# Transposes of token rows and heads' outputs by VectorE and DRAM, and weighted values in adjoining PSUM banks

## The chip, the core and the metric

The kernel runs on one core of a Trainium2 chip. The metric is the device time of one execution in microseconds. Everything is computed in float32 except for the mask, which is bfloat16. PE is TensorE, DVE is VectorE, ACT is ScalarE, POOL is GpSimd and SP is SyncE, which here only issues DMAs.

## What is computed

The input is `x` of shape (8, 1024, 128). The program applies a block twice (`DEPTH = 2`), in this order of layers as the kernel counts them (L = 0 to 3): two local-attention layers (L = 0, 1), global attention, and two more local-attention layers (L = 2, 3). Cut to what matters, one local layer is:

```python
h = shift_token(x)                       # second half of the channels comes from the token before
q, k, v = split(h @ wqkv, 3)             # 8 heads of 64
q = l2norm(q) * qs; k = l2norm(k) * ksc
q, k = rotary_xpos(q, k)
sim = einsum('bhwid,bhwjd->bhwij', 8 * q, look_around(k))    # windows of 64, this one and the one before
o = softmax(where(mask, -max, sim)) @ look_around(v)
x = x + o @ wo
h = layernorm(shift_token(x)) * g + b    # then the MLP
a, g = split(h @ w1 + b1, 2)
x = x + (a * gelu(g)) @ w2 + b2
```

Before layers 0 and 2 an outer layer norm is applied to each token row; after layers 1 and 3 half of the result is added to the residual `X`.

## The kernel before

`X` and `Y` hold all tokens in SBUF, token on the partition, as 64 rows (`NT = 64`) of 128 tokens. A local-attention stage of a layer runs in slots: `local_slot(L, s)` exists once per engine, and in slot s the engine works on several tiles of 128 tokens at once. Tile s is at the softmax, tile s+2 at the transposes of its keys and queries, tile s+3 at the values, tile s+4 at the projection of queries and keys and at its rotary products, tile s-1 at the weighted values and tile s-2 at the output projection. Each engine runs its list in a fixed order, written out by hand; semaphores alone bind the engines together. The MLP follows in groups of 4 tiles (`mlp_slot`), and the last four groups also start the next layer.

PE's order in a slot is `scores(s)`, `weigh_values(s-1)`, `heads_transpose(s-2)` (L1174), `project_qk(s+4, 0)` (L1209), `project_v(s+3)` (L1226), `project_qk(s+4, 1)`, `project_out(s-2)` (L1237), `weights_transpose(s)` twice (L1257), `tokens_transpose(s+5)` (L1164), `keys_transpose(s+2)` (L1271) and `queries_transpose(s+2)` (L1284). Token rows are transposed by TensorE to a PSUM bank and copied to `hT` by ACT in two halves (`tokens`, L536 and L537; the second half is moved by one column, which is the token shift). The outputs of the heads, `o`, are transposed by TensorE to bank 5 and copied by ACT to `oT` (`outputs`, L543).

DVE's order is `maxima(s)` (two reductions, L747), `sums(s-1)` (two reciprocals, L755), `norms(s+2)` (L771), `shares(s-1)` (two products, L762), `queries(s+4)` (sine and cosine products, L733 and L738), `add_heads(s-2)` (L799), `keys(s+4)` (cosine, sum of squares L793, sine), and in layers 0 and 2 the statistics of one row of the outer norm (`moments`, L846, L850). POOL does `root(s+4)` (floor L444, power L447), `total(s+4)` (L452) and in layers 0 and 2, for as long as there are rows, `normalise` (L464, L468, L472) for one row. `root(t)` does not start its power before `norms(t-1)` is done, and `norms(t)` needs `root(t)` and `total(t)`.

SP issues two DMAs per slot, which lay out the values of the window before (`vprev`, L393 and L395), and in slots 48, 52 and 56 of a layer `load_tokens` (L374 to L376), which copies 8 rows of `Y` for the MLP, half of the channels moved by one partition.

The weighted values of a tile lie in PSUM banks 7 and 2.

## Time and profile before

| | us |
|---|---|
| median of 3 runs | 3096.68 |
| lowest, highest | 3094.66, 3098.7 |
| profiled execution | 3094.52 |
| its span, first to last instruction | 3092.7 |

Over the span PE is busy for 3015.1 us (97%), DVE 2570.3 (83%), ACT 2223.2 (72%) and POOL 1815.0 (59%). The clock granted to TensorE is 0.991 of full speed on average. Local attention of layers 0 to 3 fills roughly 50 to 550, 680 to 1220, 1750 to 2250 and 2400 to 2930 us, global attention 1330 to 1700. Engine busy shares are unions over time; a matmul's shown duration overlaps the next one's, so throughput is read from one start to the next.

### The profile page before, as it was taken

Reading aid. Unit: us, or ns where it says so; the run is one execution under the profiler, and the core shown is the slowest. Engines: PE = TensorE matmul, PEld = TensorE weight load, DVE = VectorE, ACT = ScalarE, POOL = GpSimd, SP = SyncE. Lnnn points to the kernel's source line nnn. Section 1 sums busy time; section 2 is a strip of 40 time slices with the busy share of each in tenths; the row PEclk is TensorE's granted clock in tenths of the full one; section 3 lists DMA queues with packets and bytes.
Section 4 is the critical chain, followed back from the end, with each engine's and each line's share of the span. In section 5 each row is a group of like instructions: output and inputs, shape, how many; then the busy total and the mean of one; then the engine's idle time right before and its main releaser. Section 6 shows DMA issues by size and latency. Waiting matters only on the chain.

```text
span 3092.7 us, 83968 instructions
## 1 busy us (share of the span) xinstructions
PE 3015.1 (97%) x31009; PEld 2183.9 (71%) x31009; DVE 2570.3 (83%) x5290; ACT 2223.2 (72%) x5488; POOL 1815.0 (59%) x1258
## 2 busy tenths in 40 slices
PE   7999999999999999989999699999999999999999
PEld 4777777667777777657777477777766677777766
DVE  7999888677888888869999599999866788888866
ACT  5888888437888888328889388888853688888832
POOL 8999997125666665540000599999721566666610
PEclk8999999999999999999999899999999999999999
DMA  5111112101111121200000011111221111111211
GB/s 122 33 35 35 33 36 54 43 19 35 33 35 35 33 44 43 50 4 1 1 1 1 18 35 37 34 33 37 48 49 21 32 33 37 33 33 44 47 39 51
DMA packets 140627, 107.20 MB, mean 35 GB/s; under 512 B 85225, under 2 KB 105666, under 8 KB 140226
## 3 DMA queue, kind: packets, MB, share of 16 engines
q1 hardware_dynamic: 140226, 101.83, 14.7%
q8 instruction: 255, 4.18, 0.6%
q14 instruction: 146, 1.20, 0.1%
HBM read 12.67 MB, written 4.19 MB: 5 GB/s over the span
## 4 chain that ended last, share of the span: by engine, by line
PE 91%; DVE 4%; issue 2%; ACT 1%; POOL 1%; SPq 0%; DMA 0%; DVEq 0%; ACTq 0%; POOLq 0%
PE psum L1209 14%; PE psum L1083 11%; PE psum L1186 8%; PE psum L1226 7%; PE psum L1237 7%; PE psum L1257 7%; PE psum L1140 6%; PE psum L1109 5%; PE psum L1174 5%; PE psum L1271 3%; PE psum L1284 3%; PE psum L1470 3%; PE psum L1446 3%; PE psum L1130 3%; PE psum L1456 2%
## 5 line engine op out<-in xcount | busy, mean ns | idle before, releaser
L447 POOL TENSOR_TENSOR rnorm<-ssq_floor,neg_half 128x16 f32<-128x16 f32 x256 | 750.4, 2931 | 438.9 <-DVE qkr L771 430.0
L522 ACT ACTIVATE shared<-psum,neg_max 128x128 f32<-128x128 f32 x2048 | 595.0, 396 | 38.1 <-DVE neg_max L747 38.1
L452 POOL TENSOR_TENSOR qk_cos<-qk_cos,qk_sin 128x1024 f32<-128x1024 f32 x256 | 607.0, 2371 | 0.0
L1209 PE MATMUL psum<-wqkv,hT 128*128 128x512 f32 x1024 | 534.5, 606 | 16.8 <-DVE qk_sin L733 10.1
L733 DVE TENSOR_TENSOR qk_sin<-psum,sin 128x512 f32<-128x512 f32 x512 | 350.9, 685 | 118.3 <-ACT sq L529 117.2
L738 DVE TENSOR_TENSOR qk_cos<-psum,cos 128x512 f32<-128x512 f32 x512 | 350.7, 685 | 78.7 <-ACT sq L529 78.5
L581 ACT ACTIVATE shared<-psum,b1g 128x512 f32<-128x512 f32 (+1 forms) x192 | 131.6, 686 | 353.8 <-PE psum L1083 349.6
L543 ACT COPY shared<-psum 128x512 f32<-128x512 f32 x256 | 150.1, 586 | 322.0 <-PE psum L1174 322.0
L747 DVE TENSOR_REDUCE neg_max<-psum 128x4 f32<-128x512 f32 x512 | 327.8, 682 | 36.6 <-PE psum L1142 24.4
L529 ACT ACTIVATE sq<-psum 128x512 f32<-128x512 f32 x512 | 334.1, 653 | 27.5 <-PE psum L1209 27.3
L1083 PE MATMUL psum<-shared,w1g 128*128 128x512 f32 (+1 forms) x768 | 345.6, 593 | 5.4 <-DVE shared L837 4.0
L1237 PEld LDWEIGHTS psum<-wo,shared 128*128 128x128 f32 x2048 | 267.4, 191 | 117.8 <-issue 117.1
L771 DVE TENSOR_TENSOR qkr<-qk_cos,rnorm 128x1024 f32<-128x1024 f32 x256 | 307.7, 1202 | 19.8 <-issue 19.1
L556 ACT COPY shared<-psum 128x512 f32<-128x512 f32 x512 | 306.2, 600 | 10.7 <-PE psum L1257 5.0
L793 DVE TENSOR_REDUCE ssq<-sq 128x16 f32<-128x1024 f32 x256 | 309.3, 1208 | 0.0
L1186 PE MATMUL psum<-v,shared 128*64 128x65 f32 x4096 | 293.6, 224 | 0.0
L1189 PE MATMUL psum<-vprev,shared 128*64 128x65 f32 x4096 | 293.4, 224 | 0.0
L1186 PEld LDWEIGHTS psum<-v,shared 128*64 128x64 f32 x4096 | 258.2, 137 | 46.4 <-issue 46.4
L1226 PE MATMUL psum<-wqkv,hT 128*128 128x512 f32 x512 | 282.8, 634 | 2.1 <-DVE qk_cos L738 2.1
L1209 PEld LDWEIGHTS psum<-wqkv,hT 128*128 128x128 f32 x1024 | 178.2, 194 | 150.7 <-issue 140.9
L1257 PE MATMUL psum<-ident,shared 128*128 128x128 f32 x2048 | 270.2, 273 | 7.3 <-ACT shared L522 3.9
L1237 PE MATMUL psum<-wo,shared 128*128 128x128 f32 x2048 | 271.1, 275 | 1.5 <-ACT shared L522 1.5
(131 smaller groups left out, 6585.9 us busy)
## 6 DMA issues: line engine op xcount, KB each, us to landing
vprev<-v SPq DMA_DIRECT2D x512, 130.0 KB, 2.3
shared<-Y SPq DMA_DIRECT2D x32, 256.0 KB
shared<-Y SPq DMA_DIRECT2D x32, 254.0 KB
out<-X SPq DMA_DIRECT2D x8, 512.0 KB, 3.7
X<-in_L_attn_x SPq DMA_DIRECT2D x7, 512.0 KB, 6.9
wqkv<-in_L_ffn_wqkv SPq DMA_DIRECT2D x4, 512.0 KB, 4.1
w<-in_L_ffn_w SPq DMA_DIRECT2D x4, 341.0 KB
wqkv<-in_L_ffn_wqkv SPq DMA_DIRECT2D x4, 256.0 KB, 4.2
```

Source lines behind the costliest of these rows:

```text
L447: nc.gpsimd.tensor_tensor(rnorm[:], ssq_floor[:], neg_half[:], ALU.pow).then_inc(rnorm_ready, 1)
L452: nc.gpsimd.tensor_tensor(both, both, qk_sin[:, t.m % 2, :], ALU.add).then_inc(sum_ready, 1)
L522: last = nc.scalar.activation(probs[:, c * P:(c + 1) * P], bank(3 + i, (c % 4) * P, (c % 4 + 1) * P), ACT.Exp, bias=neg_max[:, c:c + 1])
L529: nc.scalar.activation(sq[:, i * INNER:(i + 1) * INNER], bank(i), ACT.Square).then_inc(sq_ready, 1)
L733: nc.vector.tensor_tensor(y, x[:, :, ::-1, :], part.unsqueeze(1).to_broadcast([P, HEADS, 2, DH // 2]), ALU.mult).then_inc(rot_ready, 1)
L738: nc.vector.tensor_tensor(heads(qk_cos[:, t.m % 2, i * INNER:(i + 1) * INNER]), heads(bank(i)), cos[:, t.m, i:i + 1, :].to_broadcast([P, H ...
L1083: last = nc.tensor.matmul(bank(banks[half], rows=slice(0, size)), w1g[:, half * HID + lo:half * HID + lo + size], zT, start=True, stop=True)
L1186: nc.tensor.matmul(bank(bk, col, col + HD1, slice(WIN, P)), probsT[:, at_h + WIN:at_h + P], v[:, t.m % 4, h, :], start=True, stop=True)
L1209: nc.tensor.matmul(bank(i), hT[:, t.m * P:(t.m + 1) * P], wqkv[:, i * INNER:(i + 1) * INNER], start=True, stop=True).then_inc(qk_psum, 1)
L1226: nc.tensor.matmul(bank(v_bank(t)), hT[:, t.m * P:(t.m + 1) * P], wqkv[:, 2 * INNER:3 * INNER], start=True, stop=True).then_inc(v_psum, 1)
L1237: last = nc.tensor.matmul(bank(out_bank(t), 0, P), oT[:, c * P:(c + 1) * P], wo[:, c, :], start=(c == 0), stop=(c == INNER // P - 1))
L1257: last = nc.tensor.transpose(bank(6 + i, (c % 4) * P, (c % 4 + 1) * P), probs[:, c * P:(c + 1) * P], ident[:])
```

## The change

Token rows of tiles 5 to 63 of a layer are no longer transposed by TensorE. DVE transposes the 32x32 squares of a row of `Y` where they lie (`token_blocks`), SP stores the result in a DRAM scratch tensor and loads it back in four DMAs with the squares at their transposed places, straight into `hT`. The outputs of the heads go the same way for all but the last 6 tiles of a layer (`heads_blocks`, `store_heads`, `load_heads`); DVE writes its squares so that the four channel chunks lie interleaved, and `project_out` reads its stationary operand at every fourth element. ACT's copies for these tiles go. The weighted values lie in banks 6 and 7; maxima, reciprocals and shares of a tile become one instruction each. The statistics and normalisation of the outer norm handle two rows in every second slot. The shifted copy of `load_tokens` is split into 112 and 15 partitions. Some waits follow the new owners of the banks.

```diff
+SQUARE = 32
+EARLY = 5
+LAST = 6
+    blocks_out = nc.dram_tensor("token_blocks", [4, P, P], F32).ap()
+    heads_out = nc.dram_tensor("head_blocks", [2, P, INNER], F32).ap()
+        head_blocks = shared[:, 8 * N:9 * N].rearrange("p (q n) -> p q n", q=2)
+        o_T = shared[:, 9 * N:10 * N].rearrange("p (q n) -> p q n", q=2)
+        def by_dma(t):
+            return t.row < NT - LAST
         def out_bank(t):
-            return 5 if t.row >= NT - 6 else 3
+            return 3 if by_dma(t) else 5
@@ norm_units
-            return range(s + 14, s + 15) if 0 <= s and s + 14 < NT else None
+            return range(s + 14, s + 16) if s % 2 == 0 and s + 14 < NT else None
@@ SP
-                sp.dma_start(dst[1:P, :, HALF:P], src[0:P - 1, :, HALF:P]).then_inc(done, 16)
+                sp.dma_start(dst[1:113, :, HALF:P], src[0:112, :, HALF:P]).then_inc(done, 16)
+                sp.dma_start(dst[113:P, :, HALF:P], src[112:P - 1, :, HALF:P]).then_inc(done, 16)
+            def store_heads(t):
+                k = dma_count(t)
+                sp.wait_ge(head_blocks_ready, k + 1)
+                wait(sp, heads_in[k % 2], 64 * (k // 2))
+                sp.dma_start(heads_out[k % 2], head_blocks[:, k % 2, :]).then_inc(heads_stored[k % 2], 16)
+            def load_heads(t):
+                k = dma_count(t)
+                sp.wait_ge(heads_stored[k % 2], 16 * (k // 2 + 1))
+                wait(sp, attn_ready, before(t, 2))
+                squares = heads_out[k % 2].rearrange("(b i) (j x) -> i b j x", i=SQUARE, x=P)
+                for j in range(P // SQUARE):
+                    sp.dma_start(o_T[j * SQUARE:(j + 1) * SQUARE, k % 2, :].rearrange("i (b x) -> i b x", x=P),
+                                 squares[:, :, j, :]).then_inc(heads_in[k % 2], 16)
+            def store_blocks(t):
+                k = late_count(t)
+                sp.wait_ge(blocks_ready, k + 1)
+                wait(sp, blocks_in[k % 4], 64 * (k // 4))
+                sp.dma_start(blocks_out[k % 4], blocks[:, k % 2, :]).then_inc(blocks_stored[k % 4], 16)
+            def load_blocks(t):
...
+                for j in range(P // SQUARE):
+                    lo = t.m * P + (1 if j * SQUARE >= HALF else 0)
+                    sp.dma_start(hT[j * SQUARE:(j + 1) * SQUARE, lo:lo + P].rearrange("i (b c) -> i b c", c=SQUARE),
+                                 squares[:, :, j, :]).then_inc(blocks_in[k % 4], 16)
             def local_slot(L, s):
+                if t := late_tile(L, s + 6):
+                    store_blocks(t)
+                if t := late_tile(L, s + 5):
+                    load_blocks(t)
+                if (t := tile_at(L, s - 1)) and by_dma(t):
+                    store_heads(t)
                 ... the two copies to vprev ...
+                if (t := tile_at(L, s - 1)) and by_dma(t):
+                    load_heads(t)
@@ ACT local_slot
-                if not tail and (t := tile_at(L, s - 2)):
-                    outputs(t)
                 if t := tile_at(L, s):
                     exponents(t, 0)
-                if tail and (t := tile_at(L, s - 2)):
+                if (t := tile_at(L, s - 2)) and not by_dma(t):
                     outputs(t)
-                if s >= 0 and (t := tile_at(L, s + 5)):
-                    tokens(t)
@@ DVE
             def maxima(t):
-                for i in range(2):
-                    s = bank(3 + i).rearrange("p (h k) -> p h k", k=P)
-                    wait(dve, scores_ready, before(t, 0))
-                    wait(dve, probs_ready, before(t, 1, 2))
-                    nc.vector.tensor_reduce(neg_max[:, 4 * i:4 * i + 4], s, AX_X, ALU.max,
-                                            negate=True).then_inc(max_ready, 1)
+                scored = psum[:, 3 * BANK:5 * BANK].rearrange("p (h k) -> p h k", k=P)
+                wait(dve, scores_ready, before(t, 0))
+                wait(dve, probs_ready, before(t, 1, 2))
+                nc.vector.tensor_reduce(neg_max[:], scored, AX_X, ALU.max, negate=True).then_inc(max_ready, 1)
+            def heads_blocks(t):
+                k = dma_count(t)
+                dve.wait_ge(o_ready, t.n + 1)
+                wait(dve, heads_stored[k % 2], 16 * (k // 2))
...
+                nc.vector.transpose(head_blocks[:, k % 2, :].rearrange("p (j n c) -> p j c n", j=4, c=4),
+                                    o.rearrange("p (c j n) -> p j c n", c=4, j=4)).then_inc(head_blocks_ready, 1)
+            def token_blocks(t):
...
+                if k > 1:
+                    dve.wait_ge(blocks_stored[(k - 2) % 4], 16 * ((k - 2) // 4 + 1))
+                nc.vector.transpose(blocks[:, k % 2, :], Y[:, t.row, :]).then_inc(blocks_ready, 1)
@@ DVE local_slot
                 if t := tile_at(L, s - 1):
                     shares(t)
+                    if by_dma(t):
+                        heads_blocks(t)
...
+                if t := late_tile(L, s + 7):
+                    token_blocks(t)
@@ PE
             def weigh_values(t):
-                    bk = (7, 2)[h // 4]
+                    bk = 6 + h // 4
             def project_out(t):
-                wait(pe, oT_ready, before(t, 0))
+                if by_dma(t):
+                    k = dma_count(t)
+                    pe.wait_ge(heads_in[k % 2], 64 * (k // 2 + 1))
+                    squares = o_T[:, k % 2, :].rearrange("p (x c) -> p c x", c=INNER // P)
...
+                    heads_c = squares[:, c, :] if by_dma(t) else oT[:, c * P:(c + 1) * P]
             def weights_transpose(t, i):
-                elif i == 1:
-                    wait(pe, o_ready, before(t, 1, 2))
+                else:
+                    wait(pe, o_ready, before(t, 1))
@@ PE local_slot, slots 1 to 59
                     weigh_values(tile(-1))
-                    if t := tile(-2):
-                        heads_transpose(t)
...
-                    if t := tile(5):
-                        tokens_transpose(t)
```

## Rows read from the trace of the kernel before

**Rows 1.** Stages: us; busy PE, PEld, DVE, ACT, POOL; clock, DMA share, GB/s.
```profile
200.00:300.00 100.00, 100.00 (x1258) 75.05 (x1258) 90.81 (x183) 83.01 (x229) 94.73 (x73) 1.00 0.15 34
...
2500.00:2600.00 100.00, 100.00 (x1243) 75.06 (x1243) 87.18 (x157) 83.26 (x231) 66.40 (x37) 1.00 0.15 34
```

**Rows 2.** Timeline of PE (start us, us, instruction), layer 3, one slot.
```profile
2504.75 0.66 PE L1174 MATMUL psum<-ident,shared 128*128 128x128 f32 x4
2505.24 1.02 PE L1209 MATMUL psum<-wqkv,hT 128*128 128x512 f32 x2
...
2507.90 1.05 PE L1237 MATMUL psum<-wo,shared 128*128 128x128 f32 x8
2508.79 1.04 PE L1257 MATMUL psum<-ident,shared 128*128 128x128 f32 x8
2509.66 0.27 PE L1164 MATMUL psum<-ident,Y 128*128 128x128 f32 x1
```

**Rows 3.** Timeline of DVE, layer 3, the same slot.
```profile
2503.81 1.29 DVE L747 TENSOR_REDUCE neg_max<-psum 128x4 f32<-128x512 f32 x2
...
2505.18 1.19 DVE L771 TENSOR_TENSOR qkr<-qk_cos,rnorm 128x1024 f32<-128x1024 f32 x1
2506.29 0.75 DVE L762 TENSOR_TENSOR shared<-psum,rsum 128x256 f32<-128x256 f32 x2
2507.59 0.69 DVE L733 TENSOR_TENSOR qk_sin<-psum,sin 128x512 f32<-128x512 f32 x1 [0.55 <-ACT sq L529]
2508.20 0.68 DVE L738 TENSOR_TENSOR qk_cos<-psum,cos 128x512 f32<-128x512 f32 x1
...
2510.20 1.21 DVE L793 TENSOR_REDUCE ssq<-sq 128x16 f32<-128x1024 f32 x1
2511.33 0.68 DVE L733 TENSOR_TENSOR qk_sin<-psum,sin 128x512 f32<-128x512 f32 x1
```

**Rows 4.** Timeline of POOL, layer 0, one slot and the next one's start.
```profile
203.88 2.94 POOL L447 TENSOR_TENSOR rnorm<-ssq_floor,neg_half 128x16 f32<-128x16 f32 x1
206.79 2.37 POOL L452 TENSOR_TENSOR qk_cos<-qk_cos,qk_sin 128x1024 f32<-128x1024 f32 x1
209.25 0.23 POOL L464 TENSOR_SCALAR ln_rstd<-ln_moments 128x1 f32<-128x1 f32 x1
209.56 0.58 POOL L468 TENSOR_TENSOR ln_rstd<-ln_rstd,neg_half 128x1 f32<-128x1 f32 x1
210.25 1.50 POOL L472 TENSOR_SCALAR Y<-X,ln_moments,ln_rstd 128x128 f32<-128x128 f32 x1
211.82 0.26 POOL L444 TENSOR_SCALAR ssq_floor<-ssq 128x16 f32<-128x16 f32 x1
212.16 2.93 POOL L447 TENSOR_TENSOR rnorm<-ssq_floor,neg_half 128x16 f32<-128x16 f32 x1
```

**Rows 5.** Timelines of DVE and POOL late in layer 0.
```profile
443.74 1.25 DVE L771 TENSOR_TENSOR qkr<-qk_cos,rnorm 128x1024 f32<-128x1024 f32 x1 [0.98 <-issue]
...
444.05 1.38 POOL L468 TENSOR_TENSOR ln_rstd<-ln_rstd,neg_half 128x1 f32<-128x1 f32 x1
```

**Rows 6.** Timeline of SP's issues, layer 3, two slots.
```profile
2500.80 0.46 SPq L393 DMA_DIRECT2D vprev<-v  x1
...
2509.09 0.46 SPq L393 DMA_DIRECT2D vprev<-v  x1
2509.59 0.60 SPq L395 DMA_DIRECT2D vprev<-v  x1
```

**Rows 7.** The page's DMA issues: count, KB each, median us from issue to landing.
```profile
vprev<-v SPq DMA_DIRECT2D x512, 130.0 KB, 2.3
...
out<-X SPq DMA_DIRECT2D x8, 512.0 KB, 3.7
```

**Rows 8.** Timeline of SP's issues, layer 0, slot 48.
```profile
447.40 0.68 SPq L374 DMA_DIRECT2D shared<-Y  x1
...
448.97 16.20 SPq L376 DMA_DIRECT2D shared<-Y  x1
```

More of the change, by code:

```diff
@@ L226, in macaron @@
         h_in = [sem(f"h_in{i}") for i in range(3)]
+        blocks_ready = sem("blocks_ready")
+        head_blocks_ready = sem("head_blocks_ready")
+        heads_stored = [sem(f"heads_stored{i}") for i in range(2)]
+        heads_in = [sem(f"heads_in{i}") for i in range(2)]
+        blocks_stored = [sem(f"blocks_stored{i}") for i in range(4)]
+        blocks_in = [sem(f"blocks_in{i}") for i in range(4)]
         heads = lambda t: t.rearrange("p (h d) -> p h d", d=DH)
@@ L531, in tokens @@
             def tokens(t):
-                wait(act, staged_T, before(t, 0))
+                wait(act, staged_T, early_count(t, 0))
                 wait(act, v_psum, before(t, MT - 1))
@@ L540, in outputs @@
             def outputs(t):
-                wait(act, oT_psum, before(t, 0))
+                act.wait_ge(oT_psum, last_count(t) + 1)
                 wait(act, attn_ready, before(t, 1))
@@ L750, in sums @@
+                wait(dve, scores_ready, before(t, 0))
+                wait(dve, probs_ready, before(t, 1, 2))
+                nc.vector.tensor_reduce(neg_max[:], scored, AX_X, ALU.max, negate=True).then_inc(max_ready, 1)
             def sums(t):
                 wait(dve, pv_ready, before(t, 0))
-                wait(dve, o_ready, before(t, 1, 2))
-                for i, bk in enumerate((7, 2)):
-                    pv = bank(bk, 0, 4 * HD1).rearrange("p (h d) -> p h d", d=HD1)
-                    nc.vector.reciprocal(rsum[:, 4 * i:4 * i + 4], pv[:, :, DH]).then_inc(rsum_ready, 1)
+                wait(dve, o_ready, before(t, 1))
@@ L757, in shares @@
+                nc.vector.reciprocal(rsum[:].rearrange("p (i h) -> p i h", i=2),
+                                     weighted()[:, :, :, DH]).then_inc(rsum_ready, 1)
             def shares(t):
-                dve.wait_ge(rsum_ready, 2 * t.n + 2)
-                wait(dve, oT_psum, before(t, 1))
-                for i, bk in enumerate((7, 2)):
-                    pv = bank(bk, 0, 4 * HD1).rearrange("p (h d) -> p h d", d=HD1)
-                    nc.vector.tensor_tensor(
-                        heads(o)[:, 4 * i:4 * i + 4, :], pv[:, :, 0:DH],
-                        rsum[:, 4 * i:4 * i + 4].unsqueeze(2).to_broadcast([P, 4, DH]),
-                        ALU.mult).then_inc(o_ready, 1)
+                dve.wait_ge(rsum_ready, t.n + 1)
@@ new lines, in heads_blocks @@
+            def heads_blocks(t):
+                k = dma_count(t)
+                dve.wait_ge(o_ready, t.n + 1)
+                wait(dve, heads_stored[k % 2], 16 * (k // 2))
+                if t.row == 0 and t.L == DEPTH:
+                    dve.wait_ge(out_psum, NT)
+                elif t.row == 0:
+                    wait(dve, mlp_ready, NG * t.L)
+                nc.vector.transpose(head_blocks[:, k % 2, :].rearrange("p (j n c) -> p j c n", j=4, c=4),
+                                    o.rearrange("p (c j n) -> p j c n", c=4, j=4)).then_inc(head_blocks_ready, 1)
@@ L1079, in gates @@
                     pe.wait_ge(hid_ready, 3 * t.n + c + 1 - lag)
-                if t.row == 1 and c == 1:
+                if t.row == 1 and c == 0:
+                    pe.wait_ge(hid_ready, 3 * t.n - 1)
+                elif t.row == 1 and c == 1:
                     pe.wait_ge(x1_ready, NT * (t.L + 1))
@@ L1119, in scores @@
                 wait(pe, probs_ready, before(t, 1, 2))
-                if t.row and (u := tile_at(t.L, t.row + 4)):
-                    wait(pe, hT_ready, before(u, 0, 2))
                 if t.row == 0 and t.L == DEPTH:
@@ L1152, in tokens_transpose @@
                 if x_bank(t) == 6:
[L1153 to L1155 removed]
+                    wait(pe, hT_ready, early_count(t, 1, 2))
                 elif u := tile_at(t.L, t.row - 3):
@@ L1166, in heads_transpose @@
             def heads_transpose(t):
-                wait(pe, o_ready, before(t, 0, 2))
+                wait(pe, o_ready, before(t, 0))
                 if u := tile_at(t.L, t.row + 3):
@@ L1197, in project_qk @@
                     pe.wait_ge(wqk_in, 16 * (t.L + 1))
-                wait(pe, hT_ready, before(t, 0, 2))
+                if t.row < EARLY:
+                    pe.wait_ge(hT_ready, early_count(t, 0, 2))
+                else:
+                    pe.wait_ge(blocks_in[late_count(t) % 4], 64 * (late_count(t) // 4 + 1))
                 if i == 1:
@@ L1217, in project_v @@
                     wait(pe, rot_ready, 4 * (t.n + 1) + 2)
-                elif u := tile_at(t.L, t.row - 5):
-                    wait(pe, oT_ready, before(u, 0))
+                elif u := tile_at(t.L, t.row - 2):
+                    wait(pe, qT_ready, before(u, 0))
                 else:
```

61 lines of the change are left out of this document (47 added, 14 removed).

## Prediction

> **What bounds the kernel now.** I read the table of stages first. In the middle of a local-attention stage PE is busy for all of every 100 us, in the layers with the extra layer norm (even: 0 and 2) and in those without (odd) alike [rows 1]. DVE has 91 and 87%, ACT 83%, POOL 95 and 66%. So TensorE sets the end of these stages, and POOL is next in the even layers. The same copy to `vprev` is issued at 2500.80 and at 2509.09 [rows 6]: one slot, one tile of 128 tokens, takes 8.29 us. There are 64 slots in each of four layers; the change touches some 58 of each, 232 in all.
>
> Next, PE's timeline of one slot [rows 2]. Matmuls overlap, so I count from start to start and not the 0.27 us that a single one is shown with. The four transposes of the heads' outputs (L1174) start at 2504.75 and the next line at 2505.24: 0.49 us. Eight transposes of the weights take 2508.79 to 2509.66, 0.109 us each, and the token transpose (L1164) is one more: 0.11 us. The change therefore takes 0.49 + 0.11 = 0.60 us from each slot of PE: 8.29 becomes **7.69 us**. If PE alone mattered, 232 x 0.60 = 139 us would go. The question is who stops it earlier.
>
> **DVE, odd layers.** Start to start in [rows 3]: two maxima with two reciprocals 1.37 (2503.81 to 2505.18; the maxima of 512 columns 0.60 each like the products, so 0.08 a reciprocal), norms 1.11, two shares about 0.66 (two instructions of 256 columns, shown 0.75 with the overlap), sine 0.61, cosine 0.60, the second of each 0.60, the squares' sum 1.13, the residual 0.20 (a 128-column operation beside the 512-column one at 0.60). Sum 6.88 us; the rest of the 8.29 is waiting, such as the 0.55 us for ACT before the sine. Changes: one joint maximum of 1024 columns costs as the 1024-column sum, 1.13, and one reciprocal 0.08 (-0.16 together); one 512-column product 0.60 (-0.06), but what follows now waits for its end, 0.12 more. New: the transpose of 512 columns and that of 128. No transpose of DVE is in the trace. The nearest rows are operations of one element per cycle: 0.60 start to start for 512 columns and 0.20 for 128. The other end is two cycles per element, 1.13 and 0.33. I take the lower end, because every 32-bit row of [rows 3], PSUM or SBUF, fits one element per cycle. DVE: 6.88 - 0.22 + 0.12 + 0.80 = **7.58 us**, under PE's 7.69 by only 0.1; at the upper end 8.24. A cost below nothing is excluded: the transpose is an instruction more on this engine.
>
> **DVE, even layers.** The statistics for the extra norm add what separates the two rows of [rows 1], 3.4% of 8.29 or 0.28 us, now done for two rows at a time: about **7.9 us**.
>
> **POOL, even layers.** Start to start [rows 4]: power of the norms 2.91, sum of the rotated halves 2.46, epsilon 0.31, small power 0.69, normalised row 1.57, floor 0.34: 8.28 us, the whole slot, so POOL is as full as PE. The row operation is long there (1.50 us) because it overlaps DVE's norms. Late in layer 0 the lengthening sits on another instruction: the norms run at 443.74 [rows 5], and POOL's small power beside them takes 1.38 instead of 0.58, 0.80 more. Something both engines use serialises them; I count 0.80 per such overlap. The change lets POOL prepare two rows in every second slot. A slot with rows: 2.91 + 2.46 + 0.31 + 0.85 (small power of two, the 16-column one giving 0.16 per column) + 0.80 + 0.87 + 0.34 + 0.80 of overlap = 9.34. A slot without: the next power must wait for DVE's norms, which must wait for the sum: 2.91 + 2.37 + 1.2 + about 0.2 of signalling = 6.7. Mean **8.02 us**. So in the 50 slots per even layer that have rows to prepare POOL, not PE, sets the pace. With the two engines waiting on each other there I take 8.1: 0.2 us x 100 = 20 us gained. This is where most of the 139 us goes.
>
> **ScalarE** loses the two token copies and the outputs' copy, all beside other work: worth 0. It no longer makes DVE wait 0.55 before the sine, which is the slack that DVE's additions use.
>
> **SP and the DMA queue.** A slot had two DMAs, now 12: token squares stored (1) and loaded (4), heads stored (1) and loaded (4), `vprev` (2). An issue costs 0.50 us start to start [rows 6]. After the heads' store, SP issues the two copies and then waits until the store has landed. Landing takes 2.3 us for 130 KB and 3.7 for 512 KB to DRAM [rows 7]; between them 256 KB gives 2.8. Then four loads and the next slot's five token DMAs: 2.8 + 9 x 0.50 + 0.1 = **7.4 us** per turn, below 7.69. With the ends 2.3 and 3.7 it is 6.9 and 8.3. The heads are there 0.05 + 2.8 + 1.5 + 2.3 = 6.7 us after DVE's transpose, which ends about 5.1 us into a slot; PE projects them at 5.0 of the next, 12.7: about 0.9 us to spare. Bytes are no bound: 15% of the queues moved 34 GB/s [rows 1], full use is then 225 GB/s (an estimate), and some 900 KB per slot needs 4 us of 7.7.
>
> Waits that move: the first weights' transpose now also waits for the shares, which DVE ends at 4.4 us and PE wants at 5.9; behind it stand only the keys' and queries' transposes. DVE's heads transpose waits for the shares just ahead of it; behind it are sine and cosine, for which PE's keys' transpose waits (cosine done at 6.3, wanted at 6.7). The token transpose waits for POOL's row of two slots earlier. All are covered, by 0.4 us at the thinnest.
>
> **Token pairs for the MLP.** In three slots per layer SP also issues `load_tokens`. Now the last of its DMAs holds SP for 16.20 us [rows 8]. The one before it moves 254 KB, so 16 GB/s: one engine's part of 225. The 128-partition load ahead held nobody. Split into 112 and 15 partitions the hold should go, leaving about 4 x 0.65 = 2.6 us of issue. SP's slack and the margin take half; 12 x 1.3 = 16 us lost. The page DMA: Bandwidth & Descriptors of the Trainium skill (section on why a DMA increments its semaphore by 16) says the engines used must divide the partitions, so 127 get one and 112 get 16; by that rule the hold goes, and the sum stays as it is.
>
> **Sum.** Odd layers: PE at 7.69, but with DVE 0.1 behind it I take 7.79: 0.50 x 116 = 58. Even layers, 100 slots: 20. Even layers, the 8 later slots each: 16 x 0.5 = 8. Token loads: -16. Total -70 us against the profiled execution's 3094.52 (span 3092.7), which stands 2.2 below the median of three runs: 3096.7 - 70 = **3027 us**. MLP and global attention: 0, since they keep their instructions but for a few late token squares.
>
> **Rivals.**
> *Strided weights for the projection (slower).* `project_out` takes its stationary operand at every fourth float. Its eight matmuls take 2507.90 to 2508.79, 0.11 each [rows 2]; if each load took twice as long, 0.89 is added against 0.60 removed: +0.29 x 232 = +67, about 3165 us with the token loads. It decides from 0.075 us per load upward. For it: no stationary operand in the trace is strided. Against it: loads overlap matmuls, and half of a doubled one might hide. The Trainium skill, Advanced Engine Details and Errata, section Memory Cachelines, wants at least two hits on a 16-byte line of SBUF; here each access has a line of its own, and so have DVE's strided writes. No row shows it. Chance 0.12.
> *DVE at two cycles per element.* 8.24 in odd layers, 8.6 in even: +0.27 x 100 = 27, token loads 16, small gain 6: about 3134 us. Chance 0.13. The Trainium skill (VectorE: DVE Perf Modes, The three transpose paths) gives 311 ns for a 128x128 bf16 transpose; by that the small one here is one element per cycle and the sum stands.
> *SP's turn becomes the bound.* A store landing in 3.7 us gives a turn of 8.3: no slot gains, token loads cost 16, about 3110 us. Chance 0.09. If the 16 us hold stayed, 12 x 15 = 180 us would be lost; chance 0.02.
> *All covers hold.* PE at 7.69 in odd layers, 7.95 in even, no loss at token loads: 70 + 34 + 10 = 114, about 2983 us. Chance 0.08.
> *The forecast*, 2995 to 3070: chance 0.56.
>
> **How the numbers follow.** The range, 2983 to 3130, leaves out the strided weights, the hold, and half of the DVE case. A measurement here can tell about 0.2%, 6 us, from no change. Faster: 0.56 + 0.08 + 0.03 for mild forms of the rivals = 0.67. Same 0.07. Slower 0.26.
>
> **What would show it.** L1174 gone but for six tiles per layer; a slot (`vprev` to `vprev`) of 7.7 to 7.9 us in layers 1 and 3, and about 8.1, alternating, in 0 and 2; there DVE's norms start as the sum ends. DVE's transposes 0.69 and 0.3 us. Waits of PE for DMA in `project_out` would show SP's turn; spacing above 0.11 us there, strided loads; 1.2 us transposes, the DVE rival. POOL no longer bound in even layers would prove my pairing step wrong.

## The result, and the profile after

The changed kernel takes 3190.7 us (median of four runs, 3189.6 to 3193.2) against 3097.7 beside it: ratio 1.030, interval 1.0285 to 1.032. It is 93 us slower, where 3027 us, 70 less, was forecast. The profiled execution has a span of 3187.6 us, 94.9 more than before. Some executions ran at a lower granted clock (3340.9 us at 0.846 and 11478 at 0.582 in the kernel called TensorE dense below), and the times and ratios here leave them out.

First the stages of the changed kernel (us; busy PE, PEld, DVE, ACT, POOL; clock, DMA share, GB/s), to be read beside [rows 1]:

```profile
200.00:300.00 100.00, 100.00 (x1151) 79.47 (x1151) 97.16 (x166) 70.06 (x188) 82.89 (x59) 1.00 0.42 111
900.00:1000.00 100.00, 100.00 (x1155) 78.68 (x1144) 94.83 (x141) 70.03 (x189) 63.30 (x36) 1.00 0.40 107
```

PE is still busy all of the time, at the full clock, yet it issues only 1151 matmuls in 100 us where [rows 1] have 1258. The five transposes removed were 0.60 us of a slot; what is left fills that and more. Weight loads (PEld) rose from 75 to 79% although five per slot are gone. So the time went into PE's own instructions, not into a wait. PE's timeline of one slot in layer 1 (start us, us, instruction) shows which:

```profile
903.62 1.02 PE L1316 MATMUL psum<-wqkv,hT 128*128 128x512 f32 x2
904.48 1.90 PE L1350 MATMUL psum<-wo,shared 128*128 128x128 f32 x8
906.22 1.04 PE L1370 MATMUL psum<-ident,shared 128*128 128x128 f32 x8
```

`project_out` (L1350) takes 904.48 to 906.22, 1.74 us; before it took 0.89 [rows 2]. The eight weights' transposes behind it take 0.87 us (906.22 to 907.09) as they did before. In the last slots of a layer, where the same line reads dense chunks that ScalarE has copied, it takes 0.89 in this kernel too (561.51 to 562.40). The groups of instructions (us busy, mean ns of one | idle before) say that it is the load of the stationary operand, first the group of the kernel before, which had no row of its own so far:

```profile
L1237 PEld LDWEIGHTS psum<-wo,shared 128*128 128x128 f32 x2048 | 267.4, 191 | 117.8 <-issue 117.1
```

and after:

```profile
L1350 PEld LDWEIGHTS psum<-wo,shared 128*128 128x128 f32 x2048 | 492.7, 313 | 95.1 <-issue 56.4
L1350 PE MATMUL psum<-wo,shared 128*128 128x128 f32 x2048 | 471.2, 373 | 3.0 <-DMA shared<-head_blocks 3.0
L854 DVE STREAM_TRANSPOSE shared<-shared 128x512 f32<-128x512 f32 x232 | 261.1, 1125 | 8.0
```

313 ns for one load against 191, while PE's wait for the DMA is only 3.0 us in the whole run: transport is hidden. Loads overlap one another, so what counts is the step from one to the next: 1.74 / 8 = 0.22 us against 0.11, about twice. The third line is DVE's transpose of the heads, 1.12 us where I took 0.69. DVE's timeline of a slot (as [rows 3]):

```profile
903.21 0.68 DVE L841 TENSOR_TENSOR shared<-psum,rsum 128x512 f32<-128x512 f32 x1
903.93 1.12 DVE L854 STREAM_TRANSPOSE shared<-shared 128x512 f32<-128x512 f32 x1
904.89 0.68 DVE L811 TENSOR_TENSOR qk_sin<-psum,sin 128x512 f32<-128x512 f32 x1
905.49 0.68 DVE L816 TENSOR_TENSOR qk_cos<-psum,cos 128x512 f32<-128x512 f32 x1
906.42 0.29 DVE L889 TENSOR_TENSOR Y<-psum,Y 128x128 f32<-128x128 f32 x1 [0.25 <-PE psum L1350]
...
908.95 0.30 DVE L950 STREAM_TRANSPOSE blocks<-Y 128x128 f32<-128x128 f32 x1
909.42 1.23 DVE L824 TENSOR_REDUCE neg_max<-psum 128x8 f32<-128x1024 f32 x1 [0.17 <-PE psum L1248]
```

0.96 us from its start to the sine's, and both of DVE's waits are for PE. The squares of the tokens (L950), written without a step, take 0.30 as forecast.

The slots below are worked out from the starts of DVE's norms in slots 10 and 50 of each layer, their distance divided by 40 (slots are numbered here by the tile that is normed; DVE does tile t in slot t - 2 of its list). The last column is from the norms of slot 63 to those of slot 0 of the next layer (behind layer 1 the global attention lies between).

```
                     slot of layer 0     1     2     3      layer's end to next start
before                       8.333 8.292 8.289 8.290      138.4 510.4 138.4
after                        8.555 8.557 8.555 8.555      143.4 515.5 141.7
TensorE dense                8.235 7.921 8.239 7.927      141.7 511.8 143.4
both dense                   8.013 7.713 8.017 7.707      141.7 516.9 143.3
VectorE dense                8.555 8.557 8.555 8.555      143.3 515.4 141.7
after, banks 7 and 2         8.556 8.555 8.556 8.555      140.0 513.8 140.0
TensorE at step of 8 bytes   8.231 7.923 8.234 7.923      141.7 511.8 143.4
both dense, single rows      8.090 7.708 8.089 7.706      141.7 514.9 143.3
the hold                     8.013 7.708 8.017 7.717      143.3 513.7 143.1
ScalarE places               8.335 8.090 8.382 8.130      140.0 512.0 140.0
four stores                  8.073 7.917 8.121 7.920      141.7 513.7 141.7
four stores, banks 7 and 2   8.173 7.963 8.161 8.063      140.0 508.4 140.0
pairs                        8.069 7.886 8.085 7.879      141.7 513.6 143.4
pairs, projection later      8.050 7.811 8.054 7.758      143.4 513.6 143.4
```

Of the 94.9 us, 40.7 are in slots 10 to 50 (8.9 + 3 x 10.6), 22 in slots 50 to 63, 13 in the first ten, and 18 between slot 63 and the next start or the end of the run. Even and odd layers now have the same slot: PE sets it alone, POOL no longer does.

### The profile page after: what moved, and what is told of

It reads as the page before. It is cut to its first block, busy times and chain, and to the rows that moved or that the text cites. A ratio compares the mean times of both kernels' runs of the same rounds, so it can differ in the third digit from the quotient of the medians.

```text
span 3187.6 us, 83049 instructions
## 1 busy us (share of the span) xinstructions
PE 3085.5 (97%) x29845; PEld 2314.5 (73%) x29845; DVE 2761.3 (87%) x4990; ACT 2009.2 (63%) x4784; POOL 1745.3 (55%) x1158
## 4 chain that ended last, share of the span: by engine, by line
PE 88%; DVE 4%; issue 3%; SPq 2%; DMA 1%; ACT 1%; POOL 0%; DVEq 0%; ACTq 0%; POOLq 0%
PE psum L1316 14%; PE psum L1350 13%; PE psum L1191 10%; PE psum L1290 7%; PE psum L1370 7%; PE psum L1333 6%; PE psum L1246 6%; PE psum L1217 5%; PE psum L1578 3%; PE psum L1397 3%; PE psum L1384 3%; PE psum L1554 3%; PE psum L1236 3%; PE psum L1564 2%; PE psum L1248 1%
## 5 line engine op out<-in xcount | busy, mean ns | idle before, releaser
L1316 PE MATMUL psum<-wqkv,hT 128*128 128x512 f32 x1024 | 558.1, 629 | 16.8 <-DVE qk_sin L811 10.0
L1350 PEld LDWEIGHTS psum<-wo,shared 128*128 128x128 f32 x2048 | 492.7, 313 | 95.1 <-issue 56.4
L1350 PE MATMUL psum<-wo,shared 128*128 128x128 f32 x2048 | 471.2, 373 | 3.0 <-DMA shared<-head_blocks 3.0
L639 ACT COPY shared<-psum 128x512 f32<-128x512 f32 x512 | 277.9, 593 | 253.0 <-PE psum L1370 252.9
L824 DVE TENSOR_REDUCE neg_max<-psum 128x8 f32<-128x1024 f32 x256 | 311.4, 1217 | 59.0 <-PE psum L1248 58.5
L861 DVE TENSOR_TENSOR qkr<-qk_cos,rnorm 128x1024 f32<-128x1024 f32 x256 | 300.7, 1175 | 1.1 <-PE psum L1397 0.6
L1370 PE MATMUL psum<-ident,shared 128*128 128x128 f32 x2048 | 271.8, 274 | 27.0 <-DVE shared L841 19.2
L1370 PEld LDWEIGHTS psum<-ident,shared 128*128 128x128 f32 x2048 | 260.8, 156 | 36.9 <-ACT shared L605 27.9
L854 DVE STREAM_TRANSPOSE shared<-shared 128x512 f32<-128x512 f32 x232 | 261.1, 1125 | 8.0
```

The lines of the kernel that those rows point to most:

```text
L824: nc.vector.tensor_reduce(neg_max[:], scored, AX_X, ALU.max, negate=True).then_inc(max_ready, 1)
L1316: nc.tensor.matmul(bank(i), hT[:, t.m * P:(t.m + 1) * P], wqkv[:, i * INNER:(i + 1) * INNER], start=True, stop=True).then_inc(qk_psum, 1)
L1350: last = nc.tensor.matmul(bank(out_bank(t), 0, P), heads_c, wo[:, c, :], start=(c == 0), stop=(c == INNER // P - 1))
L1370: last = nc.tensor.transpose(bank(6 + i, (c % 4) * P, (c % 4 + 1) * P), probs[:, c * P:(c + 1) * P], ident[:])
```

## The experiments

Theory A: the stationary operand of `project_out`, read at every fourth float, doubles the loads of TensorE and is the whole loss per slot; DVE's strided write costs time but is hidden beneath it. Rival B: DVE's chain sets the slot. Rival C: the layout through DRAM does, by waits or contention of transfers.

**TensorE dense.** `project_out` reads 128 adjoining floats.

```diff
-                    squares = o_T[:, k % 2, :].rearrange("p (x c) -> p c x", c=INNER // P)
+                    squares = o_T[:, k % 2, :].rearrange("p (c x) -> p c x", c=INNER // P)
```

> The changed kernel, but PE reads the heads' outputs of a chunk as 128 adjoining floats instead of every fourth (so the channels are mixed up; the work is the same in count and size). DVE still writes every fourth. Theory A (the strided stationary operand costs PE 0.85 us a slot): project_out falls back from 1.74 to 0.89 us and the slot from 8.55 to the next limit, DVE, whose operations start to start add up to 8.1 in odd layers and 8.3 on average in even ones: 8.1 to 8.35 us, and 3190 falls to about 3115 to 3140. Rival B (the project_out matmuls are slow because their operand arrives by DMA or lies beside DMA writes): project_out stays at 1.74, the time at 3190.

3087.0 us, ratio 0.997 (0.9962 to 0.9983). Slots of odd layers fall from 8.555 to 7.92. The step on TensorE is worth 104 us, more than the whole loss: without it the change is 0.3% faster than the kernel before. That is more than expected, because DVE's operations add up to less than the 8.1 us taken there. DVE's chain takes over: DVE is busy for 99.5 of 100 us in layer 1, and 7.92 is its length, 0.34 over the 7.58 forecast, of which the transpose's 0.96 - 0.60 = 0.36 accounts for all.

**VectorE dense.** Only the transpose's write is made dense.

```diff
-                nc.vector.transpose(head_blocks[:, k % 2, :].rearrange("p (j n c) -> p j c n", j=4, c=4),
+                nc.vector.transpose(head_blocks[:, k % 2, :].rearrange("p (j c n) -> p j c n", j=4, c=4),
```

> The changed kernel, but DVE writes its 32x32 squares in runs of 32 adjoining floats instead of every fourth; PE still reads every fourth (channels mixed up, same work). Theory A: DVE's large transpose falls from 1.13 to about 0.7 us, so its length came from the 16-byte step; PE is the bound, so the slot stays at 8.55 us and the time within 6 us of 3190, less 2 or 3 in the even layers. Rival (the transpose of 32-bit data is slow in itself): it stays at 1.13.

3184.2 us, ratio 1.029 (1.0269 to 1.0302), slots still 8.555. Its group of transposes reads

```profile
L854 DVE STREAM_TRANSPOSE shared<-shared 128x512 f32<-128x512 f32 x232 | 165.1, 711 | 8.0
```

711 ns in place of 1125, so the length of the transpose comes from its step and not from 32-bit data as such. The slot does not move: rival B falls for the change as made, theory A holds.

**Both dense.** Both edits at once: the machine that the prediction described.

> The changed kernel with both sides dense (channels mixed up, same work): the machine that the prediction had in mind. If its sum holds: slots of 7.7 to 7.9 us in layers 1 and 3 and 8.0 to 8.3 in 0 and 2, less the 20 us that the weights' transposes lose in the last slots of the layers: about 3027 + 20 = 3047. If SP's turn or the pairing on POOL binds instead, slots of 8.2 to 8.3 everywhere and 3110.

3041.7 us, ratio 0.983 (0.9814 to 0.9845), where 3047 was expected. Slots 7.71 and 8.01, to be held against the 7.69 (PE) and 8.02 (POOL) of the prediction. PE and POOL of this kernel:

```profile
902.99 1.05 PE L1350 MATMUL psum<-wo,shared 128*128 128x128 f32 x8
903.88 1.04 PE L1370 MATMUL psum<-ident,shared 128*128 128x128 f32 x8
```

```profile
200.32 2.93 POOL L530 TENSOR_TENSOR rnorm<-ssq_floor,neg_half 128x16 f32<-128x16 f32 x1 [1.24 <-DVE qkr L861]
...
206.81 2.38 POOL L555 TENSOR_SCALAR Y<-X,ln_moments,ln_rstd 128x128 f32<-128x128 f32 x2
...
209.62 2.93 POOL L530 TENSOR_TENSOR rnorm<-ssq_floor,neg_half 128x16 f32<-128x16 f32 x1
...
216.34 2.93 POOL L530 TENSOR_TENSOR rnorm<-ssq_floor,neg_half 128x16 f32<-128x16 f32 x1 [1.24 <-DVE qkr L861]
```

`project_out` is back at 0.89 us. POOL's slot with two rows takes 209.62 - 200.32 = 9.30 us, the one without 6.72; 9.34 and 6.7 were forecast. The 1.24 us before the power are its wait for DVE's norms. PE waits for the heads' DMA 14 times here, 17.0 us in all.

**TensorE at a step of 8 bytes.** Every second float instead of every fourth.

```diff
-                    heads_c = squares[:, c, :] if by_dma(t) else oT[:, c * P:(c + 1) * P]
+                    heads_c = squares[:, c // 2, c % 2::2] if by_dma(t) else oT[:, c * P:(c + 1) * P]
```
(with `squares` as two halves of 256 floats)

> The changed kernel with PE's stationary operand at every second float (8 bytes) instead of every fourth; channels mixed up, same work. If a 16-byte line must be hit twice, as a page of the Trainium skill has it, a load costs as little as the dense one, and the time is that of the PE-dense run, 3088. If each step beyond 4 bytes costs, project_out lies between 0.89 and 1.74 us and the time between 3088 and 3190.

3085.1 us, ratio 0.997 (0.9951 to 0.9982), slots as with dense loads:

```profile
L1350 PEld LDWEIGHTS psum<-wo,shared 128*128 128x128 f32 x2048 | 279.9, 197 | 135.2 <-issue 92.0 <-DMA shared<-head_blocks 42.5
```

197 ns a load, against 191 dense and 313 at 16 bytes. So a step of 8 bytes costs next to nothing; one float out of each 16 bytes does. This is what the Trainium skill says (Advanced Engine Details and Errata, section Memory Cachelines: at least two hits in a 16-byte line), and the runs agree with it for TensorE's loads; they don't show whether the line or something else of that size is the reason.

**Banks 7 and 2.** The changed kernel with its weighted values back in banks 7 and 2, the MLP bank that had made room for them moved back too (with it one wait went), and two reciprocals and two products for the shares. The weights' first transposes then no longer wait for the shares.

```diff
-                    bk = 6 + h // 4
+                    bk = (7, 2)[h // 4]
...
-                else:
+                elif i == 1:
                     wait(pe, o_ready, before(t, 1))
```

> The changed kernel with the weighted values back in banks 7 and 2 and their reciprocals and shares as two instructions each, so that the first weights' transpose no longer waits for the shares; strides as changed. Theory C (that wait costs some 5 us at the end of each layer): the waits of 1.6, 2.4 and 0.9 us before the weights' transposes in slots 61 to 63 go, and 3190 falls by 15 to 20 us to about 3173, slots elsewhere unchanged. Rival: the ends of the layers wait for something else as long, and the time stays within 5 us.

3178.5 us, ratio 1.027 (1.0251 to 1.0284): 12 us less than the change, where 15 to 20 was expected. The slots are unchanged; the layers' ends are shorter by 3.4, 1.7, 1.7 and, from slot 63 of layer 3 to the end, 3.3 us, 10 in all. PE at the end of layer 0 (L1257, L1370 and L1372 are the same line, the weights' transposes), before, after, and with the banks back:

```profile
555.55 0.66 PE L1257 MATMUL psum<-ident,shared 128*128 128x128 f32 x4 [0.33 <-ACT shared L522]
561.59 0.66 PE L1257 MATMUL psum<-ident,shared 128*128 128x128 f32 x4 [0.33 <-ACT shared L522]
```

```profile
568.34 0.63 PE L1370 MATMUL psum<-ident,shared 128*128 128x128 f32 x4 [1.58 <-DVE shared L841]
576.41 0.82 PE L1370 MATMUL psum<-ident,shared 128*128 128x128 f32 x4 [2.36 <-DVE shared L841]
```

```profile
574.13 0.66 PE L1372 MATMUL psum<-ident,shared 128*128 128x128 f32 x4 [1.00 <-ACT shared L605]
580.49 0.66 PE L1372 MATMUL psum<-ident,shared 128*128 128x128 f32 x4 [0.86 <-ACT shared L605]
```

In the last four slots PE has less to do ahead of this transpose (no projection of queries and keys, and `project_out` comes behind it), and the wait for the shares, covered in mid layer, is bare: 1.6 and 2.4 us. Slots 60 to 63 of every layer show the same four waits, 0.7, 1.6, 2.4 and 0.9 us; over the whole run the waits for the shares come to 19.2 us. With the banks back the wait is for ScalarE's exponents and 0.9 to 1.0 us, 11.9 us in 14 waits, against 0.33 and 3.9 us in 12 before; that rest goes with the joint maximum, which gives the exponents their first half later (argued, not tried by itself).

**Single rows.** Both dense, and POOL prepares one row in each slot, as before the change.

```diff
-            return range(s + 14, s + 16) if s % 2 == 0 and s + 14 < NT else None
+            return range(s + 14, s + 15) if 0 <= s and s + 14 < NT else None
```

> The run with both sides dense (3042), but the outer norm's rows one per slot again instead of two in every second. By the prediction's account of POOL: 2.91 + 2.46 + 0.31 + 0.69 + 0.87 + 0.34 = 7.58 us and 0.80 of overlap with DVE's norms, 8.38 a slot in layers 0 and 2 where the pairs gave 8.01: about 100 x 0.35 = 35 us more, 3077, layers 1 and 3 unchanged. Rival: pairs make no difference to POOL and the slot stays at 8.01, the time at 3042.

3046.5 us, ratio 0.984 (0.9826 to 0.9856), slots of even layers 8.09. Pairing rows gives 0.08 us a slot in the even layers. The 5 us in all are not clear of noise, the two intervals overlap; 3077 us, 35 more than with pairs, was expected. POOL's timeline shows why:

```profile
208.20 0.80 POOL L555 TENSOR_SCALAR Y<-X,ln_moments,ln_rstd 128x128 f32<-128x128 f32 x1
209.08 0.75 POOL L527 TENSOR_SCALAR ssq_floor<-ssq 128x16 f32<-128x16 f32 x1
209.92 2.94 POOL L530 TENSOR_TENSOR rnorm<-ssq_floor,neg_half 128x16 f32<-128x16 f32 x1
```

DVE's norms now fall on POOL's floor, 0.75 us instead of 0.26 [rows 4]. What the overlap adds depends on what it falls on: 0.5 here, 0.8 on the small power [rows 5]. A price taken from one instruction doesn't move with the overlap.

**The hold.** Both dense, and the token loads as before the change: one copy to 127 partitions in place of 112 and 15.

```diff
-                sp.dma_start(dst[1:113, :, HALF:P], src[0:112, :, HALF:P]).then_inc(done, 16)
-                sp.dma_start(dst[113:P, :, HALF:P], src[112:P - 1, :, HALF:P]).then_inc(done, 16)
+                sp.dma_start(dst[1:P, :, HALF:P], src[0:P - 1, :, HALF:P]).then_inc(done, 16)
```

> The run with both sides dense (3042), but the shifted copy of load_tokens as one DMA over 127 partitions again. If it holds SP for some 16 us in slots 48, 52 and 56 of each layer, the loads of heads and tokens behind it come late and PE waits: up to 12 x 15 = 180 us, 3220; at least 100 us more. If SP were free to go on, 3042.

3207.1 us (two runs), ratio 1.036 (1.0339 to 1.038), 165 us above the kernel with both dense. Slots 50 to 58 are 11.55 to 11.79 us long. The largest of PE's waits in this kernel (us in total, times, longest) is for the token squares, which stand behind the held issue:

```profile
PE psum L1315 <- DMA hT<-token_blocks: 159.7, 12, 14.2
```

That is nearly all of the 165 us. The granted clock of the run is 0.962 for the same reason: from 450 to 460 us PE is busy for 1.1 us and the clock stands at 0.50 (the 1.2 GHz level), and from 470 us on it is at 1.00 again. SP's issues in this kernel, and below them those of the changed one:

```profile
437.50 0.68 SPq L417 DMA_DIRECT2D shared<-Y  x1
438.22 0.81 SPq L418 DMA_DIRECT2D shared<-Y  x1
439.08 16.14 SPq L419 DMA_DIRECT2D shared<-Y  x1
```

```profile
532.19 0.65 SPq L417 DMA_DIRECT2D shared<-Y  x1
532.88 0.68 SPq L418 DMA_DIRECT2D shared<-Y  x1
533.60 0.93 SPq L419 DMA_DIRECT2D shared<-Y  x1
534.58 0.80 SPq L420 DMA_DIRECT2D shared<-Y  x1
```

The hold of 16.2 us [rows 8] cost nothing while SP had two issues in a slot (slots 50 to 58 took 65.3 to 66.3 us, 8 x 8.29 = 66.3); with twelve it costs 12 x 14 us. Of all the parts of the change, this split is worth most. The rows agree with the rule of the Trainium skill that the prediction cites (DMA: Bandwidth & Descriptors, section on why a DMA increments its semaphore by 16): behind 127 partitions the next issue takes 16.14 us, behind 112 and 15 it takes 0.80.

**A kernel that keeps the channels in order: ScalarE places.** DVE writes dense, ScalarE copies the loaded squares into channel order (0.64 us), TensorE reads dense; banks 7 and 2.

```diff
+                nc.scalar.copy(oT.rearrange("p (c b i) -> p c b i", c=4, b=4),
+                               o_T[:, k % 2, :].rearrange("p (b c i) -> p c b i", b=4, c=4)).then_inc(placed_ready, 1)
```

> Meant to beat both kernels with the true result: DVE writes runs of 32, the loads stay as they are, and ACT, which is free of its old copies, lays the four chunks out side by side with one copy of 512 columns, so that PE reads 128 adjoining floats; weighted values in banks 7 and 2 as in the kernel before. From the dense run (3042) and the banks run (-12): 3030, if ACT's copy hides; the heads land some 1.6 us before PE wants them in that run and the copy takes 0.6. If the copy holds ACT's exponents up, a slot grows by up to 0.6 us and the time reaches 3100 or more.

3118.8 us, ratio 1.008 (1.0067 to 1.0101), where 3030 was expected if the copy hid. The idle engine is not free of charge: PE waits for this copy, 75.9 us in all, and the squares behind it on ScalarE come later to DVE, which waits for them 37 times between 850 and 1150 us, 9.8 us in all, and not once with both dense. The waits of PE, in total us, times, longest:

```profile
PE psum L1360 <- ACT shared L633: 75.9, 116, 3.1
```

**Four stores.** The placing is left to the DMAs alone: the store is cut into four, one for each 32 partitions, and writes channel order into DRAM in runs of 128 bytes; one load of 128 partitions brings it back. Nothing has a step in SBUF.

```diff
-                sp.dma_start(heads_out[k % 2], head_blocks[:, k % 2, :]).then_inc(heads_stored[k % 2], 16)
+                out = heads_out[k % 2].rearrange("q (j n) b x -> n (q j) b x", n=SQUARE)
+                for b in range(P // SQUARE):
+                    sp.dma_start(out[:, :, b, :], head_blocks[b * SQUARE:(b + 1) * SQUARE, k % 2, :].rearrange(
+                        "n (a x) -> n a x", x=32)).then_inc(heads_stored[k % 2], 16)
```

> Here the squares of the heads' outputs stay dense on both engines (VectorE writes and TensorE reads without a step, as with both made dense), and the placing is done by the DMAs alone: the store becomes four (one for each 32 partitions, 2048 runs of 128 bytes, into channel order in DRAM), the load becomes one of 128 partitions. The SyncE queue issues as many DMAs as before. Theory (the two steps of 16 bytes are what the change loses on, and nothing else hangs on where they are removed): slots of 7.71 and 8.01 us as in the run with both dense, 3042 us, ratio 0.983. Rival: runs of 128 bytes make the store land later than the 2.0 us of one with rows of 2 KB; the load and project_out wait for it. Each us beyond the 0.9 us by which the heads were taken to be early is paid 232 times; with a store of 4 us that is 232 x 1.1 = 255, some 3300 us. Half of that would be 3170.

3097.3 us, ratio 1.001 (0.9994 to 1.0021). 55 us above the kernel with both dense: the rival's direction, at about a fifth of its size. About 23 of them are in slots 10 to 50 and 26 in slots 50 to 63, where the token loads come on top. The landing of a store is unchanged, 2.0 us, but the four issues take 2.0 where one took 0.34, so the last piece leaves some 1.5 us later. In SP's timeline of layer 1 the load is issued 3.5 us after the first store, against 2.0 in the changed kernel:

```profile
907.31 2.01 SPq L436 DMA_DIRECT2D head_blocks<-shared  x4
909.36 0.52 SPq L475 DMA_DIRECT2D vprev<-v  x1
909.92 0.60 SPq L477 DMA_DIRECT2D vprev<-v  x1
910.84 0.39 SPq L443 DMA_DIRECT2D shared<-head_blocks  x1
```

```profile
905.08 0.34 SPq L434 DMA_DIRECT2D head_blocks<-shared  x1
905.46 0.47 SPq L474 DMA_DIRECT2D vprev<-v  x1
905.97 0.60 SPq L476 DMA_DIRECT2D vprev<-v  x1
907.11 2.55 SPq L442 DMA_DIRECT2D shared<-head_blocks  x4
```

PE now does wait for the heads, `PE psum L1351 <- DMA shared<-head_blocks` with 56.7 us in 75 waits between 200 and 2900 us (16.4 in 13 with both dense), and rival C, false for the change itself, holds here. Worked out from the traces for slots 12 to 47, the heads are in SBUF 7.4 us after the end of DVE's transpose, against 6.3 with both dense: 1.9 us more until the load is issued and 0.8 less for the load, which is now one. The mean time by which they come ahead of PE falls from 1.2 to 0.4 us. The same bytes keep the DMA engines busy for 57 to 58% of the stage, 44 to 46% with both dense.

**Four stores with banks 7 and 2.**

> The first of these runs with the weighted values back in banks 7 and 2 and two instructions each for reciprocals and shares. With the change's own layout that took 12 us off, at the layers' ends, where the first weights' transpose no longer waits for the shares. Theory: the same 12 us here, 3030 us, ratio 0.978. Rival: the two further VectorE instructions (0.3 us) fill the slot of 7.71 us, where VectorE had 0.3 us to spare, and take back up to 116 x 0.2 = 23 us: 3040 to 3053.

3098.0 us, ratio 1.001 (0.9998 to 1.0017): no gain. The layers' ends are shorter again (1.7, 5.3, 1.7 us), but the slots longer by 0.04 to 0.14. That is what the rival said of DVE, which has no room for two instructions more; in the changed kernel it had, since PE set the slot. PE's waits for the heads rise too (60.1 us in 76), so DVE as the cause is likely and not shown.

**Pairs.** Channels interleaved in twos: DVE writes and TensorE reads at a step of 8 bytes, the four stores have runs of 256 bytes.

> As the run before, with channels interleaved in pairs: two VectorE transposes of 256 columns that write at a step of 8 bytes, TensorE loads at a step of 8 bytes, runs of 256 bytes in the four stores. Theory: a step of 8 bytes costs neither engine anything (TensorE was seen so), the two transposes take 2 x 0.4 us, the slots are those of the run before, 3042 us, ratio 0.983. If runs of 128 bytes are what delays the run before, this one is faster than it. If VectorE already pays at a step of 8 bytes, its two transposes take 0.55 each or more, without an effect on the slot.

3076.9 us in a single run, so without an interval, against 3095.0 beside it: some 0.6% faster. DVE's two transposes of 256 columns:

```profile
901.39 0.77 DVE L856 STREAM_TRANSPOSE shared<-shared 128x256 f32<-128x256 f32 x2
902.08 0.65 DVE L812 TENSOR_TENSOR qk_sin<-psum,sin 128x512 f32<-128x512 f32 x1
```

0.69 us start to start. The dense one, in the kernel with both dense, takes 0.64:

```profile
200.80 0.71 DVE L854 STREAM_TRANSPOSE shared<-shared 128x512 f32<-128x512 f32 x1
201.44 0.65 DVE L811 TENSOR_TENSOR qk_sin<-psum,sin 128x512 f32<-128x512 f32 x1
```

That at 16 bytes takes 0.96. On DVE, too, 8 bytes are nearly free. The DMA share of the stage falls to 0.49, and PE's waits for the heads to 36.4 us in 43. So the short runs are likely a part of what the four stores lose, and the rest their number, which wasn't tried by itself.

**Pairs, projection later.** As the one before, with `project_out` behind the slot's first four weights' transposes on PE, and its sum behind the keys' first product on DVE.

```diff
+                    weights_transpose(tile(0), 0)
                     if t := tile(-2):
                         project_out(t)
-                    weights_transpose(tile(0), 0)
                     weights_transpose(tile(0), 1)
```

> The kernel with channels in pairs, with project_out one step later on TensorE (behind the first weights' transpose of the slot, 0.87 us) and the adding of its result behind the first product of the keys on VectorE. In the kernel with pairs TensorE waited for the DMA with the heads 43 times, 36 us in all, 3.1 us at the most, and the profiled slots were 7.88 and 8.07 us. Theory (the heads come late by 0.2 to 0.8 us in most of these): 0.87 us hides most of them, the slots come near to the 7.71 and 8.01 us of the run with both dense, and the time is 3076.9 - 20 to 30 = 3045 to 3055, ratio 0.984 to 0.987. Rival (the waits are the long ones, at the layers' ends and where the queue of SyncE is behind as a whole): most of the 36 us stays, 3065 to 3077. Third: SyncE's turn is what sets the slot (6 issues in place of 3 ahead of the load), then nothing changes, 3077.

3062.1 us, ratio 0.989 (0.9875 to 0.9908): it keeps the channels in order and beats the kernel before by 33 us and the changed one by 129. PE's waits between 200 and 2900 us:

```profile
PE psum L1377 <- DVE shared L842: 26.2, 51, 2.4
PE psum L1357 <- DMA shared<-head_blocks: 18.8, 17, 2.2
```

The wait for the DMA is halved (36.4 to 18.8), but the transposes that moved ahead now wait for the shares (14.2 to 26.2). One cover was paid for in part with another, which is likely why it ends above the 3045 to 3055 expected.

## Why the prediction was wrong

- **PE's removed work** (0.60 us a slot): right. With the strides gone the slot is 7.71 against 7.69.
- **`project_out` at its old price**: the step that failed. It stood among the rivals, with the right mechanism and nearly the right price (+0.89 a slot forecast, 1.74 - 0.89 = 0.85 measured; 8.29 + 0.29 = 8.58 forecast, 8.555 measured) and a time of 3165 us, but at a chance of 0.12. (The 3165 leaves out the 16 us of token loads that it says it holds: 3096.7 + 67 + 16 = 3180.) What was held against it, that loads overlap matmuls and half of a doubled one might hide, is refuted by the trace of the kernel before. PEld is busy 75% of the time on average, but in the 0.89 us of `project_out` its loads, from the second on, stand end to end:

```profile
2507.90 0.86 PEld L1237 LDWEIGHTS psum<-wo,shared 128*128 128x128 f32 x7 [0.24 <-issue]
2508.68 0.91 PEld L1257 LDWEIGHTS psum<-ident,shared 128*128 128x128 f32 x8
```

A longer load had next to nothing beneath which to hide. The chance should have been set by that; that no load in the trace was strided spoke neither for nor against a price.
- **DVE's large transpose**: the term was mis-sized, 0.96 us start to start against 0.60. Neither end of the bracket was the reason; the write at 16 bytes was (0.64 dense). Hidden behind PE in the change, it is the bound once TensorE is dense (7.92). In its place 7.58 was forecast; 7.58 + 0.36 = 7.94.
- **POOL's pairs**: the sums of both slots were right (9.30 and 6.72), the reason partly not: single rows cost 8.09, hardly more. In the changed kernel POOL no longer matters, since PE is slower than it.
- **SP's turn**: right. In the timeline of the changed kernel it starts at 905.08 and its last issue ends at 912.20 (910.23 + 1.97), 7.1 us, against 7.4. The heads' store lands in 2.0 us, not 2.8, and the four loads take 2.55 us to issue, not 2.0. PE has the heads 1.2 us early with both dense, where about 0.9 was forecast.
- **Token loads**: the hold goes, as forecast. The stretch of slots 50 to 58 costs 3.7, 2.1, 2.8 and 3.5 us more, 12.1 in all where 8 x 0.26 x 4 = 8 belong to the slots as such; so some 4 us for the extra issues and not 16. With both dense, where the shorter slots leave SP less slack, the same stretches are 11 us longer than 8 slots each, so 16 was not far off for the machine that was forecast.
- **Covers**: "all are covered, by 0.4 us at the thinnest" was worked out from a slot in mid layer. In the last four slots of a layer there is no projection of queries and keys ahead (and one of values in the first of them alone), and the wait for the shares is bare. 12 us measured with the banks back, for a term put at nothing; the layers' ends are 18 us longer than before. They are 18 us longer with both dense too, with 18.9 us of waits for the shares, and 3041.7 lies 15 above 3027; that it is these waits wasn't tried in that kernel. The cover called thinnest, cosine ahead of the keys' transposes, also failed there: 24.4 us in 56 waits of PE, none of them between 850 and 1150 us in layer 1.
- **The sum.** Against the forecast the change is 164 us slower. A dense read on TensorE takes back 104 of them, a dense write on DVE, once that is done, 45 more, and 15 remain. Against the kernel before, the slots give +0.265 x 232 = 61 us (0.85 for TensorE's loads less 0.60 for what was removed is 0.25 of the 0.265) and the banks 12; the other some 20 are spread over the first and last slots of the layers, where the joint maximum, the DMAs' start and the longer loads meet. They weren't separated.

## What to carry to other kernels

A layout that saves instructions elsewhere is priced first at its readers: a stationary operand or a transposed write that takes one float of every 16 bytes costs nearly twice and half as much again here, two floats of every 16 bytes cost next to nothing. Whether a longer load can hide is read from the loads of that one line, not from the average: at 75% over the slot they stood end to end where it mattered. A wait that is covered in the steady state must be checked in the slots at the ends of a loop, where the covering work is missing.

## What the runs showed of the hardware

- 128x128 f32 stationary operand: load 191 ns dense, 197 at a step of 8 bytes, 313 at 16 bytes; eight loads with their matmuls of 128 columns take 0.89 and 1.74 us.
- DVE's f32 transpose in squares of 32: 128x512 0.71 us (0.64 start to start) dense, 1.12 (0.96) with a write at 16 bytes; 128x128 0.30.
- Behind a copy in 127 partitions the next issue held SP for 16.1 us; behind 112 and 15 partitions it took 0.80, and the two themselves 1.7 (532.88 to 534.58).
- A store of 256 KB to DRAM lands in 2.0 us, as do four of 64 KB; each issue of the latter takes SP 0.5 us, that of the former 0.34.
- Two of POOL's instructions were longer beside DVE's norms, the floor by 0.5 us (0.26 to 0.75) and the small power by 0.8 (0.58 to 1.38).
- While PE stood idle behind the held issue (busy for 1.1 us of 450 to 460), the granted clock was 0.50; from 470 us on, with PE busy again, it was 1.00.
